# Attention outputs stored as the accumulator leaves them, divided by their sums in the output projection

## The chip, the cores and the metric

The kernel runs on one core of one Trainium2 chip. The metric is the device time of one execution in microseconds. Before the change it is 2662.52 us, the median of 3 runs (2662.07 to 2663.43).

## What is computed

The input x is [4, 2048, 256] in fp32. With xn its layer norm, the result is x + attention(xn) + ffn(xn). The feed-forward part quantises activations and weights to FP4 in blocks of 16 and is not touched. Attention has 16 heads of 16 elements, rotary positions and a causal mask:

```python
q = _rope(q); k = _rope(k)
scores = jnp.einsum('bhqd,bhkd->bhqk', q, k) * scale
scores = jnp.where(causal, scores, jnp.finfo(scores.dtype).min)
attn = jax.nn.softmax(scores, axis=-1)
out = jnp.einsum('bhqk,bhkd->bhqd', attn, v)
return out.transpose(0, 2, 1, 3).reshape(B, S, D) @ Wo.T
```

## The kernel before

Three stages follow each other, each a block of its own in which all engines start together. norm_ffn_qkv leaves x plus the feed-forward result in SBUF (x_all) and q, k, v in DRAM. attention leaves one output per head group in DRAM (oscr). out_projection multiplies by Wo, adds x_all and stores.

Attention has 16 iterations: 4 groups of 4 heads times 4 batches. The queries of an iteration form 4 blocks of 512. For each block of keys at or under the diagonal there is a step. TensorE writes transposed scores (128 keys x 512 queries) for 4 heads into 3 banks (L1013, with a mask matmul at L1018 on the diagonal), ScalarE takes exponentials (L1089), and TensorE weighs v with them into one accumulator bank (L1033). Each head fills 32 rows of it, 16 of values and 16 that hold the sum of the weights, since v is padded with ones.

Softmax needs a row maximum first. TensorE computes the scores a second time, queries as rows, into a ring of 4 banks ("tile", L988), and VectorE reduces them (L1161, with the mask L1166). The maxima are split into three bf16 parts by GpSimd, turned by TensorE (L999), copied by VectorE (L1183), and placed by SyncE as extra rows of q (L929). Part of these tiles belongs to the next iteration.

When a block's accumulator is complete, ScalarE copies it to acc_sb (L1094). TensorE turns it with four transposes into a bank of the same ring (L1043). VectorE takes reciprocals of the sums (L1190) and multiplies (L1193), and SyncE stores 128 x 256 values (L921). This is an "out".

A string of letters, ORDER, sets one order that all engines follow: s is the next score or weighing step, t the next tile of the maxima, r the turn of a row, o an out. Each engine takes from this plan what concerns it. SyncE's queue follows it too, and each DMA waits there in order.

The last stage loads 512 rows of outputs at a time (L1258), turns each 128 x 256 tile with two transposes (L1287), ScalarE copies it (L1313), TensorE projects it with two fp32 matmuls (L1295), VectorE adds x_all (L1329), SyncE stores (L1270). Loads wait until the tile before has been turned.

## Time and profile before

| | |
|---|---|
| profiled execution | 2663.43 us |
| its span | 2661.6 us |
| TensorE matmul busy | 2495.5 us (94%) |
| VectorE busy | 2259.2 us (85%) |
| ScalarE busy | 1629.7 us (61%) |
| GpSimd busy | 73.4 us (3%) |
| mean DMA rate | 59 GB/s |

The span is what the profile covers of the execution; the time is a little longer. In the profile PE is TensorE's matmul, PEld its weight loads, DVE VectorE, ACT ScalarE, POOL GpSimd and SPq SyncE's queue. A busy TensorE is a modelled value, since matmuls are pipelined: one starts before the one ahead has ended. Distances between starts say what it really takes. fp32 matmuls leave two records each, transposes one.

### The profile page before, as it was taken

The numbers are of one execution on the slowest core, as the hardware profiler recorded it, in microseconds if no ns is written. First come the engines' busy times: TensorE is split into PE (matmuls) and PEld (weight loads), VectorE is DVE, ScalarE is ACT, GpSimd is POOL, SyncE is SP. The second block draws the span as 40 slices with busy tenths as digits, with TensorE's granted clock in tenths as the row PEclk, the third lists the DMA queues.
The fourth block names the chain that finished last, engine by engine and source line by source line (L and its number), as shares of the span: only waits on it lengthen the run. The fifth ranks groups of instructions, "written<-read, shape, count | busy, mean of one in ns | idle before, by whom it ended". The sixth has DMA issues, their size and how long they took to land. (4 is left out here: it accounts for less than half of the span.)

```text
span 2661.6 us, 55085 instructions
## 1 busy us (share of the span) xinstructions
PE 2495.5 (94%) x14690; PEld 1210.8 (45%) x14690; DVE 2259.2 (85%) x4939; ACT 1629.7 (61%) x3325; POOL 73.4 (3%) x263
## 2 busy tenths in 40 slices
PE   3699999999998799999999999999999999999979
PEld 1355555655555144344344344444444443433337
DVE  6889889889998798898888889888888988988803
ACT  2355445454553077777777777777777777767752
POOL 0000000000000100000000000000000000000000
PEclk9799999999999599999999999999999999999999
DMA  5021112112211502111112112012011111110017
GB/s 183 32 71 57 65 67 71 58 60 71 71 50 67 140 26 64 28 53 59 36 47 65 30 53 65 23 59 63 26 59 44 44 59 30 51 53 6 7 41 216
DMA packets 168616, 157.81 MB, mean 59 GB/s; under 512 B 47216, under 2 KB 147312, under 8 KB 168432
## 3 DMA queue, kind: packets, MB, share of 16 engines
q1 hardware_dynamic: 168288, 155.10, 19.2%
q8 instruction: 114, 1.87, 0.3%
q14 instruction: 70, 0.57, 0.1%
q10 hardware_dynamic: 144, 0.26, 0.0%
HBM read 95.81 MB, written 58.72 MB: 58 GB/s over the span
## 5 line engine op out<-in xcount | busy, mean ns | idle before, releaser
L1089 ACT ACTIVATE prob<-score 128x512 f32<-128x512 f32 (+3 forms) x2560 | 1158.6, 542 | 472.0 <-PE score L1018 252.1
L1161 DVE TENSOR_REDUCE top<-tile 128x1 f32<-128x512 f32 x1536 | 956.5, 682 | 98.8 <-PE tile L988 92.0
L1013 PE MATMUL score<-qs,ks 99*128 99x512 bf16 (+3 forms) x2560 | 810.9, 351 | 7.1 <-ACT prob L1089 3.1
L988 PE MATMUL tile<-ks,qs 96*128 96x512 bf16 (+3 forms) x2560 | 785.9, 356 | 22.7 <-DMA ks<-qkp 14.8
L1033 PE MATMUL acc<-prob,vs 128*32 128x512 f32 (+3 forms) x5120 | 537.9, 535 | 0.0
L1166 DVE CUSTOM_DVE_ANT_0 tile<-tile,mask 128x128 f32<-128x128 f32 (+3 forms) x1024 | 471.3, 520 | 57.1 <-PE tile L988 41.1
L1013 PEld LDWEIGHTS score<-qs,ks 99*128 99x128 bf16 x2560 | 246.3, 97 | 395.8 <-ACT prob L1089 209.1
L988 PEld LDWEIGHTS tile<-ks,qs 96*128 96x128 bf16 x2560 | 236.3, 98 | 318.4 <-DVE top L1161 101.5
L362 PE MATMUL gu<-wguT,xT 128*128 128x512 f32 (+1 forms) x768 | 315.0, 563 | 20.1 <-DVE hid L670 20.1
L1033 PEld LDWEIGHTS acc<-prob,vs 128*32 128x32 f32 x5120 | 130.3, 109 | 242.9 <-issue 139.3
L362 PEld LDWEIGHTS gu<-wguT,xT 128*128 128x128 f32 x768 | 145.2, 193 | 167.7 <-issue 125.2
L1018 PE MATMUL score<-identb,maskb 128*128 128x128 bf16 x1024 | 214.6, 221 | 3.4 <-issue 3.4
L398 PE MATMUL misc<-wdT,hT 128*128 128x256 f32 x768 | 184.8, 392 | 1.3 <-ACT hT L463 1.3
L398 PEld LDWEIGHTS misc<-wdT,hT 128*128 128x128 f32 x768 | 148.4, 197 | 33.1 <-issue 11.3
L1166 DVE DVE_READ_ACCUMULATOR2_ANT top<- 128x1 f32 x1024 | 143.5, 140 | 1.7 <-issue 1.7
L386 PE MATMUL misc<-xT,wqkvT_sb 128*128 128x512 f32 x256 | 119.3, 610 | 7.6 <-ACT xT L463 7.6
L1018 PEld LDWEIGHTS score<-identb,maskb 128*128 128x128 bf16 x1024 | 101.2, 99 | 48.0 <-issue 2.5
L468 ACT ACTIVATE magic<-scaled 128x704 f32<-128x704 f32 (+1 forms) x96 | 71.1, 741 | 74.4 <-DVE scaled L124 74.4
L483 ACT ACTIVATE silu<-gu 128x704 f32<-128x704 f32 x64 | 48.4, 757 | 102.3 <-PE gu L362 102.3
L133 DVE SCALAR_TENSOR_TENSOR scaled<-magic,scaled 128x704 f32<-128x704 f32 (+1 forms) x96 | 78.7, 820 | 30.4 <-ACT magic L468 29.8
L463 ACT COPY hT<-misc 128x512 f32<-128x512 f32 (+1 forms) x128 | 58.1, 482 | 64.4 <-PE misc L394 63.8
L394 PE MATMUL misc<-identf_sb,hq 128*128 128x128 f32 x384 | 59.5, 278 | 33.3 <-DVE hq L137 28.0
(101 smaller groups left out, 1739.3 us busy)
## 6 DMA issues: line engine op xcount, KB each, us to landing
qkp<-parts SPq DMA_DIRECT2D x192, 128.0 KB
vscr<-vt SPq DMA_DIRECT2D x16, 1024.0 KB, 4.5
vs<-vscr SPq DMA_DIRECT2D x16, 1024.0 KB, 5.7
qs<-qkp SPq DMA_DIRECT2D x64, 192.0 KB, 3.4
ks<-qkp SPq DMA_DIRECT2D x64, 192.0 KB, 3.4
x_all<-in_x SPq DMA_DIRECT2D x16, 512.0 KB, 8.9
qs<-qkp SPq DMA_DIRECT2D x64, 128.0 KB, 3.1
ks<-qkp SPq DMA_DIRECT2D x64, 128.0 KB, 3.1
```

Source lines behind the costliest of these rows:

```text
L133: link(nc.vector.scalar_tensor_tensor(out=scaled, in0=magic, scalar=1.25 * MAGIC, in1=scaled, op0=ALU.max, op1=ALU.add))
L362: mm = nc.tensor.matmul(gu[:, t % 2, c0:c0 + w], xT[:, KT + k, t * P:(t + 1) * P], wguT[:, k, c0:c0 + w], start=(k == 0), stop=(k == KT - 1))
L386: mm = nc.tensor.matmul(bank, wqkvT[:, k, t * P:(t + 1) * P], xT[:, k, :], start=(k == 0), stop=(k == KT - 1))
L398: mm = nc.tensor.matmul(bank[:, 0:DIM], hT[:, t % 2, i, :], wdT[:, i, :], start=(i == 0), stop=(i == IT - 1))
L468: nc.scalar.activation(magic[:, par, 0:w], scaled[:, par, 0:w], ACT.Abs, scale=MAGIC).then_inc(magic_ready, 1)
L988: mm = nc.tensor.matmul(bank[:, h * width:(h + 1) * width], qs[par][0:ROWS, h0 + h, q0:q0 + P], ks[par][0:ROWS, h0 + h, k0:k0 + width], st ...
L1013: mm = nc.tensor.matmul(bank[:, 0:width], ks[par][0:ROWS_M, h, kb * P:(kb + 1) * P], qs[par][0:ROWS_M, h, qb * GROUP + off:(qb + 1) * GROU ...
L1018: mm = nc.tensor.matmul(bank[:, 0:P], maskb[:], identb[:], start=False, stop=True, skip_group_check=True)
L1033: mm = nc.tensor.matmul(acc[h * VW:(h + 1) * VW, off:GROUP], vs[par][:, kb // GT, kb % GT, h, :], prob[:, (HG * n + h) % PROB_SLOTS, 0:GRO ...
L1089: nc.scalar.activation(prob[:, k % PROB_SLOTS, 0:width], score[:, k % SCORE_SLOTS, 0:width], ACT.Exp, scale=HEAD ** -0.5).then_inc(probs_r ...
L1161: nc.vector.tensor_reduce(top[:, j, h0, c:c + 1], bank, AX.X, ALU.max).then_inc(tile_taken, 1)
L1166: last = nc.vector.tensor_tensor_reduce(out=head, in0=head, in1=mask[:, GROUP - width:GROUP], scale=1.0, scalar=MASK, op0=ALU.add, op1=ALU ...
```

## The change

The accumulator goes to DRAM as it is: 128 rows (4 heads x 32) by 512 queries. acc_sb has two halves, and ScalarE's copy waits until the store of two blocks before has landed. Transposes, reciprocal, product and the ring bank of an out are gone. At the letter o only SyncE does something: it stores.

In the last iteration, behind the store of block 1, SyncE loads into the buffers qs0 and ks0, which are free by then, the sums of three batches (12 DMAs) and the turned outputs of 6 of the 16 groups (24 DMAs). When VectorE is through with its iteration it takes the reciprocals of 64 x 1536 sums. GpSimd splits them into three bf16 parts in four passes. After its last store SyncE writes the parts to DRAM and reads those of two batches back as 48 rows, heads times parts.

The last stage starts with the sums of the fourth batch. ScalarE issues the loads of the other 10 groups, 40 DMAs, with no wait. Per group TensorE spreads the reciprocals over 128 rows (two matmuls with a 0/1 matrix of 48 rows), VectorE multiplies the turned outputs by them (2 x 128x512), TensorE projects (8 matmuls), and VectorE adds. There are 4 result buffers in place of 2, and no loop.

```diff
-ORDER = ("stsststtsttssststststsssstststsstssrtsssttstssotststsstsststststtstsststssststststssttsstsssstst"
...
+ORDER = ("stssttsststtssttsstsssstsststsststsssrtststststststostssstststssttststststsststssttsstststssstss"
...
-    uses = [e for e in plan if e[0] in ("tile", "row", "out") and (more or e[0] == "out" or not e[-1])]
+    uses = [e for e in plan if e[0] in ("tile", "row") and (more or not e[-1])]
...
+SUM_ROWS, SPLIT, LAST = QB * HEADS, (BATCH - 2) * QB, (BATCH - 1) * QB
+def load_sums(sp, d, dst, b, loaded):
+    for qb in range(QB):
+        src = d["oscr"][:, b * QB + qb].rearrange("h (k r) c -> h k r c", r=VW)[:, :, HEAD, :]
+        sp.dma_start(dst[qb * HEADS:(qb + 1) * HEADS, :], src).then_inc(loaded, 16)
+def batch_recips(d, p, batches):
+    return d["rscr"][p, batches].rearrange("b g h c -> (g h) b c")
+def turned_groups(flat):
+    return [flat[:, n:n + KT * GROUP].rearrange("p (k c) -> p k c", c=GROUP) for n in range(0, flat.shape[1], KT * GROUP)]
+def load_turned(eng, d, dst, g, k, loaded):
+    for h in range(HGS // KT):
+        src = d["oscr"][k * HGS // KT + h, g].rearrange("(k r) c -> k r c", r=VW)[:, 0:HEAD, :]
+        rows = slice(h * HG * HEAD, (h + 1) * HG * HEAD)
+        eng.dma_start(dst[rows, k, :], src).then_inc(loaded, 16)
+def load_recips(eng, d, recips, b, loaded):
+    for p in range(PARTS):
+        eng.dma_start(recips[p * HEADS:(p + 1) * HEADS], d["rscr"][p, b].rearrange("q h c -> h q c")
+                      ).then_inc(loaded, 16)
+def split_recips(pool, nc, links, base, rest, parts):
+    nc.gpsimd.tensor_copy(parts[0], rest).then_inc(links, 1)
+    pool.wait_ge(links, base + 1)
+    nc.gpsimd.tensor_tensor(rest, rest, parts[0], ALU.subtract).then_inc(links, 1)
+    pool.wait_ge(links, base + 2)
+    nc.gpsimd.tensor_copy(parts[1], rest).then_inc(links, 1)
+    pool.wait_ge(links, base + 3)
+    return nc.gpsimd.tensor_tensor(parts[2], rest, parts[1], ALU.subtract)
...
-        qs = [sb(f"qs{i}", [P, HG, SEQ], BF16) for i in range(2)]
-        ks = [sb(f"ks{i}", [P, HG, SEQ], BF16) for i in range(2)]
+        qs = [qs0, sb("qs1", [P, HG, SEQ], BF16)]
+        ks = [ks0, sb("ks1", [P, HG, SEQ], BF16)]
-        acc_sb = sb("acc_sb", [P, GROUP])
-        recip = sb("recip", [P, GT * HG])
-        ot = sb("ot", [P, 2, GT * HG, HEAD])
+        acc_sb = sb("acc_sb", [P, 2, GROUP])
+        sum_parts = sb("sum_parts", [SUM_ROWS, PARTS, BATCH - 1, GROUP], BF16)
...
-            def store(it, more, e):
-                n, _ = place(it, more, e)
+            def store(it, e):
                 qb = e[1]
-                await_on(sp, sp_passed, tile_taken, n + 1 + TILE_SLOTS)
+                await_on(sp, sp_passed, acc_taken, it * QB + qb + 2)
                 dst = d["oscr"].rearrange("h g p c -> (h g) p c")[ds(it * QB + qb, 1)]
-                sp.dma_start(dst.rearrange("a p c -> (a p) c"),
-                             ot[:, qb % 2].rearrange("p t e -> p (t e)")).then_inc(out_stored[qb % 2], 16)
+                sp.dma_start(dst.rearrange("a p c -> (a p) c"), acc_sb[:, qb % 2, :]).then_inc(out_stored[qb % 2], 16)
                     elif e[0] == "out":
-                        store(it, more, e)
+                        store(it, e)
+                        if more is False and e[1] == 1:
+                            for stored in out_stored:
+                                await_on(sp, sp_passed, stored, it * (QB // 2 * 16) + 1)
+                            await_on(sp, sp_passed, scores_ready, it * HEAD_STEPS)
+                            for b in range(BATCH - 1):
+                                load_sums(sp, d, sums[:, b, :], b, sums_loaded)
+                            for g, dst in enumerate(ahead):
+                                for k in range(KT):
+                                    load_turned(sp, d, dst, g, k, ahead_loaded)
+            await_on(sp, sp_passed, pick_ready, 1)
+            await_on(sp, sp_passed, recips_split, 1)
+            for p in range(PARTS):
+                sp.dma_start(batch_recips(d, p, slice(0, BATCH - 1)), sum_parts[:, p, :, :]).then_inc(recips_stored, 16)
+            await_on(sp, sp_passed, recips_stored, PARTS * 16)
+            for b in range(BATCH - 2):
+                load_recips(sp, d, recips[:, b * QB:(b + 1) * QB, :], b, recips_loaded)
...
-            def out_turn(it, more, e):
-                pe.wait_ge(acc_taken, it * QB + e[1] + 2)
-                bank = tile_slot(it, more, e)
-                for t in range(GT):
-                    mm = nc.tensor.transpose(bank[:, t * P:(t + 1) * P], acc_sb[:, t * P:(t + 1) * P], identf[:])
-                mm.then_inc(tile_full, 1)
...
             def take_acc(it, e):
                 act.wait_ge(pv_done, it * STEPS + e[1] + 1 + PROB_STEPS)
-                nc.scalar.copy(acc_sb[:], acc[:]).then_inc(acc_taken, 1)
+                qb = e[2]
+                act.wait_ge(out_stored[qb % 2], it * (QB // 2 * 16) + qb // 2 * 16 + 1)
+                nc.scalar.copy(acc_sb[:, qb % 2, :], acc[:]).then_inc(acc_taken, 1)
...
+            pool.wait_ge(recips_ready, 1)
+            split_recips(pool, nc, pool_links, ITERS * QB * TOP_LINKS, sums, [sum_parts[:, p] for p in range(PARTS)]
+                         ).then_inc(recips_split, 1)
-            def normalise(it, more, e):
-                qb = e[1]
-                dve.wait_ge(tile_taken, place(it, more, e)[0] + TILE_SLOTS)
-                sums = tile_bank(it, more, e).rearrange("p (t e) -> p t e", e=VW)
-                link(nc.vector.reciprocal(recip[:], sums[:, :, HEAD]))
-                dve.wait_ge(out_stored[qb % 2], it * (QB // 2 * 16) + qb // 2 * 16 + 1)
-                nc.vector.tensor_tensor(ot[:, qb % 2], sums[:, :, 0:HEAD],
-                                        recip[:].unsqueeze(2).broadcast_to([P, GT * HG, HEAD]),
-                                        ALU.mult).then_inc(tile_taken, 1)
...
+            dve.wait_ge(sums_loaded, (BATCH - 1) * QB * 16)
+            nc.vector.reciprocal(sums, sums).then_inc(recips_ready, 1)
+def out_projection(nc, d, x_all, woT, ahead, pickb, recips, out):
+    FIRST = len(ahead)
+    Y_SLOTS = 4
+        spread = ctx.enter_context(nc.psum_tensor("o_spread", [P, 2, KT, GROUP], F32))
+        prod = ctx.enter_context(nc.psum_tensor("o_prod", [P, GT, 512], F32))
+        later = sb("later", [P, (GROUPS - FIRST) * KT * GROUP])
+        attT = ahead + turned_groups(later[:])
+        last_recips = sb("last_recips", [PARTS * HEADS, GROUPS - SPLIT, GROUP], BF16)
+        scaledT = [sb(f"scaledT{i}", [P, KT, GROUP]) for i in range(2)]
+        y = [sb(f"y{i}", [P, GT, DIM]) for i in range(Y_SLOTS)]
...
-            def load(g, par):
-                for h in range(HGS):
-                    src = d["oscr"][h, ds(g, 1)].rearrange("a p (t e) -> p (a t) e", e=OUTW)
-                    sp.dma_start(att[par][:, :, h * OUTW:(h + 1) * OUTW], src).then_inc(att_loaded[par], 16)
...
+            load_sums(sp, d, sums[:], BATCH - 1, sums_loaded)
+            load_recips(sp, d, last_recips[:, 0:QB, :], BATCH - 2, recips_loaded[0])
+            for g in range(GROUPS):
+                if g == 2:
+                    sp.wait_ge(recips_split, 1)
+                    for p in range(PARTS):
+                        sp.dma_start(batch_recips(d, p, slice(BATCH - 1, BATCH)).rearrange("p b c -> p (b c)"),
+                                     sum_parts[:, p, :]).then_inc(recips_stored, 16)
+                if g == 4:
+                    sp.wait_ge(recips_stored, PARTS * 16)
+                    load_recips(sp, d, last_recips[:, QB:2 * QB, :], BATCH - 1, recips_loaded[1])
+                sp.wait_ge(prod_taken, (g + 1) * GT)
+                sp.dma_start(rows[g], y[g % Y_SLOTS][:]).then_inc(y_stored[g % Y_SLOTS], 16)
+            for stored in y_stored:
+                sp.wait_ge(stored, GROUPS // Y_SLOTS * 16)
+        @block.scalar
+        def _(act):
+            for g in range(FIRST, GROUPS):
+                for k in range(KT):
+                    load_turned(act, d, attT[g], g, k, att_loaded[g - FIRST])
+            def spread_recips(g):
+                if g >= SPLIT:
+                    pe.wait_ge(recips_loaded[(g - SPLIT) // QB], PARTS * 16)
+                if g >= 2:
+                    pe.wait_ge(scaled_ready, (g - 1) * KT)
+                recip = recips[:, g, :] if g < SPLIT else last_recips[:, g - SPLIT, :]
                 for k in range(KT):
-                    mm = nc.tensor.transpose(turned[:, t % 2, k * P:(k + 1) * P],
-                                             att[par][:, t % GT, k * P:(k + 1) * P], identf[:])
-                mm.then_inc(turn_full, 1)
-            def project(i, t):
-                pe.wait_ge(turn_taken, i * PAIR + t + 1 + 2)
-                pe.wait_ge(prod_taken, i * PAIR + t + 1)
+                    nc.tensor.matmul(spread[:, g % 2, k, :], pickb[:, k * P:(k + 1) * P], recip,
+                                     start=True, stop=True).then_inc(spread_full, 1)
+            def project(g, t):
+                pe.wait_ge(scaled_ready, (g + 1) * KT)
+                if g:
+                    pe.wait_ge(prod_taken, (g - 1) * GT + t + 1)
                 for k in range(KT):
-                    mm = nc.tensor.matmul(prod[:, t % 2, 0:DIM], attT[:, t % 2, k * P:(k + 1) * P], woT[:, k, :],
+                    mm = nc.tensor.matmul(prod[:, t, 0:DIM], scaledT[g % 2][:, k, t * P:(t + 1) * P], woT[:, k, :],
                                           start=(k == 0), stop=(k == KT - 1))
                 mm.then_inc(prod_full, 1)
+            spread_recips(0)
+            for g in range(GROUPS):
+                if g + 1 < GROUPS:
+                    spread_recips(g + 1)
+                for t in range(GT):
+                    project(g, t)
...
+            def scale(g):
+                if g >= FIRST:
+                    dve.wait_ge(att_loaded[g - FIRST], HGS * 16)
+                if g >= 2:
+                    dve.wait_ge(prod_full, (g - 1) * GT)
+                for k in range(KT):
+                    dve.wait_ge(spread_full, g * KT + k + 1)
+                    nc.vector.tensor_tensor(scaledT[g % 2][:, k, :], attT[g][:, k, :], spread[:, g % 2, k, :],
+                                            ALU.mult).then_inc(scaled_ready, 1)
+            scale(0)
+            scale(1)
+            dve.wait_ge(sums_loaded, QB * 16)
+            nc.vector.reciprocal(sums[:], sums[:]).then_inc(recips_ready, 1)
+            for g in range(GROUPS):
+                if g >= Y_SLOTS:
+                    dve.wait_ge(y_stored[g % Y_SLOTS], g // Y_SLOTS * 16)
+                for t in range(GT):
+                    dve.wait_ge(prod_full, g * GT + t + 1)
+                    nc.vector.tensor_tensor(y[g % Y_SLOTS][:, t, :], prod[:, t, 0:DIM], x_all[:, g * GT + t, :],
                                             ALU.add).then_inc(prod_taken, 1)
+                if g + 2 < GROUPS:
+                    scale(g + 2)
...
+            q_flat, k_flat = (buf[:].rearrange("p h c -> p (h c)").bitcast(F32) for buf in (qs0, ks0))
+            half = k_flat.shape[1] // 2
+            ahead = turned_groups(q_flat) + turned_groups(k_flat[:, 0:half])
+            sums = k_flat[0:SUM_ROWS, half:half + (BATCH - 1) * GROUP].rearrange("p (b c) -> p b c", c=GROUP)
```

The places that the prediction speaks of follow as rows of each engine's program. TensorE in attention, before and after, from the tiles between the accumulators of blocks 1 and 2 on:

```order
L988 MATMUL tile<-ks,qs 128x512
L1011 REGISTER_ALU
L1013 MATMUL score<-qs,ks 128x512
L974 REGISTER_ALU
L1043 MATMUL tile<-identf_sb,acc_sb 128x128 x4
L974 REGISTER_ALU
L988 MATMUL tile<-ks,qs 128x384
```

```order
L1061 MATMUL tile<-ks,qs 128x512
L1084 REGISTER_ALU
L1086 MATMUL score<-qs,ks 128x512
L1084 REGISTER_ALU
L1086 MATMUL score<-qs,ks 128x512
L1047 REGISTER_ALU
L1061 MATMUL tile<-ks,qs 128x384
```

The four transposes of the out are gone, and nothing waits there for the copy. VectorE at the same place, before and after:

```order
L1161 TENSOR_REDUCE top<-tile 128x1
L1188 REGISTER_ALU
L1154 REGISTER_ALU
L1190 RECIPROCAL recip<-tile 128x16
L1193 TENSOR_TENSOR ot<-tile,recip 128x256
L1154 REGISTER_ALU
L1166 ISA tile,top<-tile,mask 128x384
```

```order
L1230 TENSOR_REDUCE top<-tile 128x1
L1223 REGISTER_ALU
L1230 TENSOR_REDUCE top<-tile 128x1
L1223 REGISTER_ALU
L1235 ISA tile,top<-tile,mask 128x384
```

Reductions and masked reductions follow each other directly. SyncE's queue from the last iteration's outs to the first loads of the last stage, before and after:

```order
L921 DMA oscr<-ot 128x256 x2
L929 DMA qs<-row 3x4x128 x4
L921 DMA oscr<-ot 128x256 x2
L839 UNCONDITIONAL_BRANCH
L1251 UNCONDITIONAL_BRANCH
L1258 DMA att<-oscr 128x4x64 x8
```

```order
L975 DMA oscr<-acc_sb 128x512 x2
L823 DMA ks<-oscr 16x1x512 x12
L843 DMA qs<-oscr 64x1x512 x16
L843 DMA ks<-oscr 64x1x512 x8
L982 DMA qs<-row 3x4x128 x4
L975 DMA oscr<-acc_sb 128x512 x2
L1034 DMA rscr<-sum_parts 64x3x512 x3
L849 DMA recips<-rscr 16x4x512 x6
L887 UNCONDITIONAL_BRANCH
L1315 UNCONDITIONAL_BRANCH
L823 DMA last_sums<-oscr 16x1x512 x4
```

36 loads now stand ahead of the row of block 3, and nine DMAs and two waits for landings stand behind the last store.

## Rows read from the trace of the kernel before

**Rows 1.** Table of stretches, busy us (instructions) of PE, PEld, DVE, ACT, POOL; clock, DMA, GB/s:

```profile
1143.00:1245.70 102.70, 102.08 (x726) 42.48 (x726) 92.22 (x242) 75.73 (x166) 4.02 (x16) 1.00 0.17 48
...
2581.30:2586.40 5.10, 4.96 (x14) 3.80 (x15) 0.42 (x1) 1.12 (x3) 0.00 (x0) 0.50 0.34 76
2586.40:2661.60 75.20, 69.09 (x371) 57.99 (x369) 26.76 (x63) 22.04 (x61) 0.00 (x0) 1.00 0.75 209
```

**Rows 2.** Timeline of ScalarE, two accumulator copies (start us, us, instruction):

```profile
1143.04 0.59 ACT L1094 COPY acc_sb<-acc 128x512 f32<-128x512 f32 x1 [0.19 <-PE acc L1033]
...
1348.39 0.59 ACT L1094 COPY acc_sb<-acc 128x512 f32<-128x512 f32 x1 [0.19 <-PE acc L1033]
```

**Rows 3.** Timeline of TensorE around an out in attention:

```profile
1504.10 0.60 PE L1043 MATMUL tile<-identf_sb,acc_sb 128*128 128x128 f32 x4
1504.53 0.38 PE L1013 MATMUL score<-qs,ks 99*128 99x512 bf16 x1
1504.75 0.38 PE L988 MATMUL tile<-ks,qs 96*128 96x512 bf16 x1
...
1505.50 1.92 PE L1033 MATMUL acc<-prob,vs 128*32 128x512 f32 x16
1507.36 0.34 PE L988 MATMUL tile<-ks,qs 96*128 96x384 bf16 x1
```

**Rows 4.** Timeline of VectorE around the same out:

```profile
1504.38 1.27 DVE L1161 TENSOR_REDUCE top<-tile 128x1 f32<-128x512 f32 x2
...
1506.50 0.68 DVE L1161 TENSOR_REDUCE top<-tile 128x1 f32<-128x512 f32 x1
```

**Rows 5.** Waits between 1100 and 2300 us (total us, times, longest):

```profile
PE tile L1043 <- ACT acc_sb L1094: 5.5, 12, 0.5
```

**Rows 6.** Timelines of the last iteration, SyncE's queue and TensorE:

```profile
2507.80 0.33 SPq L921 DMA_DIRECT2D oscr<-ot  x1
2526.96 2.98 SPq L929 DMA_DIRECT2D qs<-row  x4
...
2532.13 0.84 PE L1013 MATMUL score<-qs,ks 99*128 99x512 bf16 x3
```

**Rows 7.** SyncE's issues by line: ns min/median/max, first and last start:

```profile
L929 SPq DMA_DIRECT2D qs<-row x256: 697/699/841, 892.3 to 2529.2; - x128
L899 SPq DMA_DIRECT2D ks<-qkp x192: 563/583/1545, 874.2 to 2366.2; - x192
L921 SPq DMA_DIRECT2D oscr<-ot x64: 332/361/374, 941.6 to 2574.3; - x64
```

**Rows 8.** From attention to the last stage: timeline rows and one of the chain:

```profile
2572.13 0.59 ACT L1094 COPY acc_sb<-acc 128x512 f32<-128x512 f32 x1 [0.55 <-PE acc L1033]
...
2578.36 2.84 DMA att<-oscr
...
2582.55 2.08 PE L1295 MATMUL o_prod<-woT_sb,attT 128*128 128x256 f32 x4
```

**Rows 9.** A projection on the chain that ended last, and the last addition:

```profile
2604.30 0.87 PE o_prod L1295 x4
...
2657.86 0.42 DVE L1329 TENSOR_TENSOR y<-o_prod,x_all 128x256 f32<-128x256 f32 x1 [0.44 <-PE o_prod L1295]
```

**Rows 10.** Groups by line and shape: busy us, mean ns, idle time before:

```profile
L124 DVE SCALAR_TENSOR_TENSOR scaled<-xn,inv 128x512 f32<-128x512 f32 x32 | 22.1, 692 | 1.1
L1190 DVE RECIPROCAL recip<-tile 128x16 f32<-128x16 f32 x64 | 16.5, 257 | 57.6 <-PE tile L1043 52.3
L104 DVE RECIPROCAL inv<-inv 128x96 f32<-128x96 f32 x1 | 0.8, 753 | 0.0
L1329 DVE TENSOR_TENSOR y<-o_prod,x_all 128x256 f32<-128x256 f32 x64 | 27.2, 425 | 56.9 <-PE o_prod L1295 55.3 <-DMA out<-y 1.6
L1131 POOL TENSOR_TENSOR top_parts<-rest,top_parts 128x16 bf16<-128x16 f32 x64 | 17.1, 267 | 11.5 <-POOL top_parts L1129 11.5
L544 POOL MEMSET vt<- 128x2048 f32 x1 | 1.8, 1805 | 0.3 <-POOLq L1378 0.3
```

**Rows 11.** DMA issues by line: KB each, median us to landing:

```profile
vs<-vscr SPq DMA_DIRECT2D x16, 1024.0 KB, 5.7
```

More of the change, by code:

```diff
@@ L50 @@
 ITERS = HGS * BATCH
-OUTW = HG * HEAD
-OT = GT * OUTW
 LEAD = 0.52
@@ L814, in slot_free, with attention @@
     return it * per_iteration + last - per_iteration + 1 + slots
-def attention(nc, d, identf):
+SUM_ROWS, SPLIT, LAST = QB * HEADS, (BATCH - 2) * QB, (BATCH - 1) * QB
[24 more added lines that the diff above has]
+    return nc.gpsimd.tensor_tensor(parts[2], rest, parts[1], ALU.subtract)
+def attention(nc, d, identf, qs0, ks0, ahead, sums, pickb, recips):
     plan, STEPS = attention_plan()
@@ L1059, in iteration @@
                         weigh(it, i, par, e)
-                    elif e[0] == "out":
-                        out_turn(it, more, e)
                     elif e[0] == "tile" and (more or not e[-1]):
@@ L1203, in _ @@
                     take_row(None, None, e)
-            assert not link.n
             def iteration(it, more):
-                link.enter(it * OUT_LINKS)
                 for e in plan:
-                    if e[0] == "out":
-                        normalise(it, more, e)
-                    elif e[0] == "tile" and (more or not e[-1]):
+                    if e[0] == "tile" and (more or not e[-1]):
                         reduce_tile(it, more, e)
@@ L1253, in _ @@
             rows = out.rearrange("(g t p) k -> g p t k", t=GT, p=P)
-            def load(g, par):
-                for h in range(HGS):
-                    src = d["oscr"][h, ds(g, 1)].rearrange("a p (t e) -> p (a t) e", e=OUTW)
-                    sp.dma_start(att[par][:, :, h * OUTW:(h + 1) * OUTW], src).then_inc(att_loaded[par], 16)
-            load(0, 0)
-            load(1, 1)
-            def pair(i, more):
-                for par in range(2):
-                    if more:
-                        await_on(sp, sp_passed, turn_full, i * PAIR + GT * (par + 1) + 2)
-                        load(i * 2 + 2 + par, par)
-                    await_on(sp, sp_passed, prod_taken, i * PAIR + GT * (par + 1) + 2)
-                    sp.dma_start(rows[ds(i * 2 + par, 1)].rearrange("a p t k -> p (a t) k"), y[par][:]
-                                 ).then_inc(y_stored[par], 16)
@@ L1297, in project @@
                 mm.then_inc(prod_full, 1)
-            with pe.Fori(0, GROUPS // 2) as i:
-                for t in range(PAIR):
-                    turn(i, t)
-                    if t:
-                        project(i, t - 1)
-                project(i, PAIR - 1)
-        @block.scalar
-        def _(act):
-            with act.Fori(0, GROUPS // 2) as i:
-                for t in range(PAIR):
-                    act.wait_ge(turn_full, i * PAIR + t + 1 + 2)
-                    act.wait_ge(prod_full, i * PAIR + t + 1)
-                    nc.scalar.copy(attT[:, t % 2, :], turned[:, t % 2, 0:DIM]).then_inc(turn_taken, 1)
+            spread_recips(0)
@@ L1315, in _ @@
+            for g in range(GROUPS):
[3 more added lines that the diff above has]
+                    project(g, t)
         @block.gpsimd
         def _(pool):
-            for s, n in ((turn_full, 2), (turn_taken, 2), (prod_full, 2), (prod_taken, 2), (y_stored[0], 1),
-                         (y_stored[1], 1)):
-                pool.sem_inc(s, n)
+            pool.wait_ge(recips_ready, 1)
+            split_recips(pool, nc, split_links, 0, sums[:], [sum_parts[:, p, :] for p in range(PARTS)]
+                         ).then_inc(recips_split, 1)
@@ L1340, in program @@
         norm_ffn_qkv(nc, d, x_all, woT, identf)
-        attention(nc, d, identf)
-        out_projection(nc, d, x_all, woT, identf, out)
+        with nc.sbuf_tensor("qs0", [P, HG, SEQ], BF16) as qs0, nc.sbuf_tensor("ks0", [P, HG, SEQ], BF16) as ks0, \
+                nc.sbuf_tensor("pickb", [PARTS * HEADS, DIM], BF16) as pickb, \
+                nc.sbuf_tensor("recips", [PARTS * HEADS, SPLIT, GROUP], BF16) as recips:
+            q_flat, k_flat = (buf[:].rearrange("p h c -> p (h c)").bitcast(F32) for buf in (qs0, ks0))
+            half = k_flat.shape[1] // 2
+            ahead = turned_groups(q_flat) + turned_groups(k_flat[:, 0:half])
+            sums = k_flat[0:SUM_ROWS, half:half + (BATCH - 1) * GROUP].rearrange("p (b c) -> p b c", c=GROUP)
+            attention(nc, d, identf, qs0, ks0, ahead, sums, pickb, recips)
+            out_projection(nc, d, x_all, woT, ahead, pickb, recips, out)
 def constants():
```

74 lines of the change are left out of this document (35 added, 39 removed).

## The prediction

> **What bounds the kernel now.** The order of reading was: the table of stretches, the timelines of TensorE and VectorE inside attention, the waits, then the end. The table gives one steady iteration of attention: 102.70 us with TensorE busy 102.08, VectorE 92.22, ScalarE 75.73 [rows 1]. The copy of the last block's accumulator stands at 1143.04 and two iterations later at 1348.39 [rows 2], so one takes 205.35 / 2 = 102.7 us. There are 16, some 1640 of the 2661.6 us; from the last accumulator copy [rows 8] to the span's end are 89.5.
>
> TensorE's busy time is modelled, so its load is counted from distances between starts. A 512-column bf16 matmul follows the next after 0.22 us (1504.53 to 1504.75), the sixteen records of two weighing steps take 1.86 (1505.50 to 1507.36), the four transposes 0.43 (1504.10 to 1504.53) [rows 3]. Per iteration scores and maxima have 69,632 columns each, 272 x 0.22 = 59.8 us; 64 mask matmuls at a quarter of that, 3.5; 24 full weighing steps x 0.93 = 22.3; 16 diagonal ones at 5/8 of the columns, 9.3; four out-turns, 1.7. That is 96.6 of 102.7: TensorE truly idles 6 us, VectorE 10.5. Neither is the bound alone; they meet in a ring of four banks, and VectorE runs dry while TensorE weighs. The two floors are close, so removed work counts only in part.
>
> After attention, the last accumulator copy starts at 2572.13 and the first projection at 2582.55 [rows 8]; then 64 tiles follow until the last addition at 2657.86 [rows 9], 75.3 us, TensorE bound: four projection records take 0.87 [rows 9] and two transposes 0.22, 1.09 a tile against 75.3 / 64 = 1.18 measured.
>
> **Part 1: attention loses the out-turn.** Each of 64 blocks loses four transposes on TensorE (0.43 us) and a reciprocal and a product on VectorE. On VectorE two reductions run from 1504.38 for 1.27 and the next starts only at 1506.50 [rows 4]: the pair occupies 2.12 - 1.27 = 0.85 us. If TensorE alone bounds, the gain is 63 x 0.43 = 27 us, plus its waits for the copy before a transpose, 5.5 us in 1200 [rows 5], 7 us in all: 27 to 34. If VectorE alone bounds, 60 x 0.85 = 51 us and, with the slot hand-overs around it, at most 55. TensorE is the nearer to full, so I start from its 34 and add 6: VectorE's relief is 3.4 us an iteration, which is twice TensorE's own 1.7, so some of TensorE's 6 us of waiting for a bank or a probability goes too. I take 40 us, 2.5 an iteration, ends 27 and 55. The new order of letters keeps 200 steps of scores and weighing and 140 tile letters; runs of three tiles fall from 6 to 5 and runs of two rise from 17 to 22. I price it at nothing, with ends inside those of this part and one rival. The last two outs lie in the last iteration, where VectorE is free.
>
> ScalarE's copy now waits for the store of two blocks before. Behind it on ScalarE stand all exponentials. The store is issued as soon as the copy is done, its issue costs 0.36 us [rows 7], and two blocks later is 31 us or more on, apart from the short block 0; I cost it at nothing. SyncE's store waits for the copy instead of VectorE, so it is earlier.
>
> **Part 2: SyncE's queue in the last iteration.** After the store of block 1, 12 small loads and 24 of 128 KB are issued ahead of the row of block 3. Before, this gap went from 2507.80 to 2526.96, 19.2 us, the scores that need the row start at 2532.13, and the row's own four issues take 2.98 [rows 6]. The trace has no such issue; its neighbours are 0.36, 0.58 and 0.70 us [rows 7], so 36 take 13, 21 or 25 us. The store itself now comes some 3 us earlier. At 0.58 the row is placed in time; at 0.70 it is 3 us late and eats the slack. Taken 0, ends 0 and 5 us.
>
> **Part 3: the reciprocals of three batches.** SyncE places the last row at 2526.96 [rows 6], right behind VectorE's last copy of the iteration, so VectorE is free from 2527. A reciprocal costs 257 ns for 16 elements and 753 for 96 [rows 10], 6.2 ns each; 1536 elements take 9.7 us, done by 2537. Then four GpSimd passes over 64 x 1536. GpSimd shows 267 ns for 16 elements and 1805 for a fill of 2048 [rows 10]. Scaled by length, that is 1.4 us or 25.6 us a pass, 5 to 102 in all. I take the row of near length, doubled for the second operand, some 11 us. SyncE asks for the result near 2573, so 36 us are free and anything up to 9 us a pass costs nothing. The Trainium skill, "GPSIMD Engine Reference", section 3.1, gives 4497 ns for a two-input fp32 pass over 2048; as an estimate from that page a pass here takes 3.4 us and four 13.5, also hidden. No row here shows it.
>
> **Part 4: the hand-over.** From the start of the copy: copy 0.6, store issue 0.4, three reciprocal stores at 0.58 (1.7), landing 2.8 as the load at 2578.36 [rows 8], six loads at 0.58 (3.5), less one overlap, landing 2.8, block change 0.3: about 11 us, so TensorE starts near 2583. It spreads two halves at half speed (0.44 each; the granted clock was 0.50 between 2581.3 and 2586.4, the 1.2 GHz level, after 8 us without work [rows 1]) and VectorE scales them, 0.69 us each, the price of a 512-column fp32 pass [rows 10]. First projection at 2585.2, 2.7 us later than before; ends 1 and 5.
>
> **Part 5: the last stage.** Per group TensorE has 2 x 0.22 for spreading and 4 x 0.87, 3.92 us against 4.71 measured now (75.3 / 16). VectorE has 2 x 0.69 + 4 x 0.43 = 3.1, beside it. ScalarE leaves the path. But VectorE does a reciprocal of 64 x 512 between its second scaling and the first addition: 257 ns + 496 x 6.2 = 3.3 us, after sums that land near 2587.3, so until 2590.7. Group 0 has four product banks, so TensorE stands until 2591.2. Then 15 groups x 3.92 less a spreading already done = 58.4 us, so the last addition starts near 2649.5 against 2657.86. Gain of parts 4 and 5 together, rounded for the waits between: 8.5 us, ends 4 and 12.
>
> **Sum.** 40 + 8.5 = 48.5 us off the profiled execution's 2663.43, 2614.9; that execution is 0.9 above the median of 2662.52, so about 2614 as a median. What a measurement here can tell from no change is about 0.2%, 5 us.
>
> **Rivals.**
> TensorE alone is the bound in attention, VectorE's relief only lengthens its idle time: 27 + 8.5, so 2627. For it: 96.6 of 102.7 filled. Against: the waits for banks.
> VectorE's slot counts whole: 55 + 8.5, so 2599. For it: each weighing step leaves TensorE ahead by its ring only. Against: VectorE idles 10.5 us already.
> The last stage becomes bound by transfers: it now asks for 40 loads x 128 KB = 5.2 MB from ScalarE's queue at once, beside 8.4 MB of results. At the 209 GB/s of the present stage [rows 1] that is 65 us, just what TensorE needs. At 1024 KB in 5.7 us, 184 GB/s [rows 11], it is 74, and the stage gains nothing: 2623. Against: DMA was busy 0.75 with rows of 256 bytes, now they are 2 KB. The Trainium skill, "DMA: Bandwidth & Descriptors", section "Issuing engines are not separate DMA queues", says that DMAs issued from several engines share the same 16 engines and save only issue time. By that rule the loads from ScalarE slow the stores of SyncE, and this rival is more likely than two queues suggest.
> The new order loses what the lighter engines win (2.5 us an iteration more waiting at the ring): 8.5 only, 2654.
> On the other side: the GpSimd split is slow. At 25.6 us a pass it ends near 2639, 66 us after SyncE asks, and the second split (64 x 512, a third of it, 34 us) then holds SyncE at group 2 with the results of that group, some 20 us more with four result buffers. 2662.5 - 48.5 + 66 + 20 = 2700. It decides from 9 us a pass on, and makes the kernel slower from some 20. For it: GpSimd's only arithmetic rows are short. Against: its fill of 2048 elements ran at 0.9 ns each.
>
> **How the numbers follow.** Forecast 0.56, TensorE alone 0.16, VectorE whole 0.11, transfers 0.07, order 0.04, GpSimd 0.06. The predicted time is 2614. The likeliest case has 2603 to 2624; the range reaches to 2597 for the VectorE case and to 2636 for TensorE alone with a late row and a late hand-over, leaving out the order and GpSimd cases. Faster by over 0.2%: all but the last and part of the order case, 0.91; within: 0.03; slower: 0.06.
>
> **What would show it.** The distance of the accumulator copies over two iterations should fall from 205.35 to about 200.4. VectorE busy per iteration should be near 89.5 and TensorE's idle time between 5 and 6. The GpSimd passes over 1536 elements should take 1.4 to 5 us and end before the last copy. First projection 13 us after the start of the last copy. Groups in the last stage 3.9 us apart, with one gap of 1 to 3 us before group 1. Wrong would be: groups over 4.3 apart with VectorE waiting for loads or stores, a TensorE wait for the row of block 3 in the last iteration, or an iteration above 101.5.

## The result and the profile after

The changed kernel takes 2654.45 us, the median of 10 runs (2652.05 to 2657.97); the kernel before took 2662.29 beside it. The ratio is 0.9971, 95% interval 0.9961 to 0.9981. It is faster by about 8 us, where 48.5 were forecast and 2597 was the range's lower end, 2636 its upper.

The account needs three marks: the copy of block 3's accumulator in the last iteration but one, the last copy, the span's end.

| | before | after | gained |
|---|---|---|---|
| copy of block 3, iteration 14 (from 0) | 2473.27 | 2441.44 | 31.8 |
| from there to the last copy | 98.9 | 115.6 | -16.7 |
| last copy to the span's end | 89.5 | 96.8 | -7.3 |
| span | 2661.6 | 2653.8 | 7.8 |

The first mark before, in ScalarE's timeline:

```profile
2473.27 0.59 ACT L1094 COPY acc_sb<-acc 128x512 f32<-128x512 f32 x1 [0.55 <-PE acc L1033]
```

Timeline of ScalarE after, the two copies that answer to [rows 2], and those of the account:

```profile
1138.18 0.58 ACT L1162 COPY acc_sb<-acc 128x512 f32<-128x512 f32 x1 [0.19 <-PE acc L1106]
1339.62 0.58 ACT L1162 COPY acc_sb<-acc 128x512 f32<-128x512 f32 x1 [0.19 <-PE acc L1106]
2441.44 0.58 ACT L1162 COPY acc_sb<-acc 128x512 f32<-128x512 f32 x1 [0.71 <-PE acc L1106]
2557.05 0.58 ACT L1162 COPY acc_sb<-acc 128x512 f32<-128x512 f32 x1 [0.55 <-PE acc L1106]
```

An iteration of attention takes 201.44 / 2 = 100.7 us against 102.7: 2 us gained of the 2.5 forecast. Of the 40.7 us that are missing from the forecast gain of 48.5, 8.2 are missing in the first line of the table (31.8 instead of 40), 16.7 in the second, and 15.8 in the third (a loss of 7.3 instead of a gain of 8.5). SyncE's queue after, in the last iteration, which answers to [rows 6] (start us, us from the first issue's start to the last one's end, count):

```profile
2472.85 0.33 SPq L975 DMA_DIRECT2D oscr<-acc_sb  x1
2473.43 8.18 SPq L823 DMA_DIRECT2D ks<-oscr  x12
2481.66 13.61 SPq L843 DMA_DIRECT2D qs<-oscr  x16
2495.31 10.24 SPq L843 DMA_DIRECT2D ks<-oscr  x8
2505.67 3.46 SPq L982 DMA_DIRECT2D qs<-row  x4
```

The 36 loads hold the queue for 32 us. VectorE had the row of block 3 ready at 2494.33, but SyncE placed it from 2505.67 on. Its last issue ends at 2509.13, and TensorE goes on only at 2515.90. VectorE's and TensorE's timelines, and the wait between 2441 and 2557 us:

```profile
2494.05 0.28 DVE L1252 CAST row<-tile 48x128 bf16<-48x128 f32 x1 [5.91 <-PE tile L1072]
2515.90 1.46 PE L1086 MATMUL score<-qs,ks 99*128 99x512 bf16 x3 [16.83 <-DMA qs<-row]
```

```profile
PE score L1086 <- DMA qs<-row: 16.8, 1, 16.8
```

So the row is late twice: 11.3 us in being issued, and then, between the last issue's end and the scores, 6.8 us, where r_major (below) needs 1.1 (2501.36 to 2502.45). What moves in most of that time is the loads. DMA traffic after between 2509.13 and 2514.5 us (packets, MB, share of 16 engines):

```profile
q1 hardware_dynamic: 283, 0.55, 26.3%
```

In the trace's packets the last 2 KB of the loads end at 2514.83, and the row's own packets, of 256 bytes, run from 2514.56 to 2514.96. The 16.8 us are nearly all of the second line of the table: in loads_behind (below), which has no such wait, the last iteration takes 97.6 us. Another 1 us or so goes behind the wait, where the granted clock is 0.50, the 1.2 GHz level, until 2519.4.

In the last stage the issues of the same load by line (ns min/median/max, first and last start), then DMA issues of that stage (KB each, median us to landing) and a wait:

```profile
L843 ACTq DMA_DIRECT2D later<-oscr x40: 537/1799/4024, 2567.9 to 2630.8; - x40
L843 SPq DMA_DIRECT2D qs<-oscr x16: 528/548/1384, 2481.7 to 2494.1; - x16
L843 SPq DMA_DIRECT2D ks<-oscr x8: 1164/1208/1452, 2495.3 to 2504.4; - x8
```

```profile
out<-y SPq DMA_DIRECT2D x16, 512.0 KB, 8.5
```

```profile
DVE scaledT L1385 <- DMA later<-oscr: 11.9, 3, 4.7
```

ScalarE needs 62.9 us from the first to the last start of 40 issues, so the last loads come late. On the chain that ended last stands one of these loads, `later<-oscr`, with 13.65 us to landing.

### The profile page after: what moved, and what is told of

Its sections match the earlier page's. It is cut to its first block and busy times, and to the rows that moved or that the text cites. A ratio compares the mean times of both kernels' runs of the same rounds, so it can differ in the third digit from the quotient of the medians.

```text
span 2653.8 us, 53527 instructions
## 1 busy us (share of the span) xinstructions
PE 2456.0 (93%) x14338; PEld 1176.3 (44%) x14338; DVE 2250.4 (85%) x4845; ACT 1603.0 (60%) x3262; POOL 85.9 (3%) x271
## 5 line engine op out<-in xcount | busy, mean ns | idle before, releaser
L1086 PE MATMUL score<-qs,ks 99*128 99x512 bf16 (+3 forms) x2560 | 815.0, 351 | 39.3 <-DMA qs<-row 16.8
L1061 PE MATMUL tile<-ks,qs 96*128 96x512 bf16 (+3 forms) x2560 | 776.8, 355 | 23.0 <-DMA ks<-qkp 14.2
L396 PEld LDWEIGHTS misc<-wdT,hT 128*128 128x128 f32 x768 | 149.4, 198 | 33.1 <-issue 11.3
```

The lines of the kernel that those rows point to most:

```text
L396: mm = nc.tensor.matmul(bank[:, 0:DIM], hT[:, t % 2, i, :], wdT[:, i, :], start=(i == 0), stop=(i == IT - 1))
L1061: mm = nc.tensor.matmul(bank[:, h * width:(h + 1) * width], qs[par][0:ROWS, h0 + h, q0:q0 + P], ks[par][0:ROWS, h0 + h, k0:k0 + width], st ...
L1086: mm = nc.tensor.matmul(bank[:, 0:width], ks[par][0:ROWS_M, h, kb * P:(kb + 1) * P], qs[par][0:ROWS_M, h, qb * GROUP + off:(qb + 1) * GROU ...
```

## The experiments

All kernels start from the changed one, except where said. "Iteration" is the distance of two block-3 copies two iterations apart, halved. The kernel before took 2661.11 us beside them (2662.29 beside the changed kernel). Iterations and the last column are read from the profiled execution of each run.

| run | us | ratio to before, 95% | iteration | last copy to end of span |
|---|---|---|---|---|
| changed kernel | 2654.45 | 0.9971 [0.9961, 0.9981] | 100.7 | 96.8 |
| r_major | 2630.75 | 0.9887 [0.9870, 0.9903] | 100.7 | 86.1 |
| loads_behind | 2638.90 | 0.9916 [0.9900, 0.9933] | 100.7 | 96.2 |
| two_heads_load, one run | 2710.39 | | 100.7 | 152.7 |
| old_order | 2678.68 | 1.0064 [1.0047, 1.0081] | 102.2 | 97.1 |
| new_order_before | 2666.84 | 1.0017 [1.0007, 1.0026] | 103.1 | 89.2 |
| dve_back, one run | 2664.96 | | 101.6 | 96.9 |
| pe_back, one run | 2706.81 | | 102.7 | 115.8 |
| repaired | 2620.39 | 0.9846 [0.9833, 0.9859] | 100.7 | 80.6 |

**r_major: the axis order of one load.** The 128 KB load walks its source as 4 heads x 16 rows x 512. Here the rows come first, with the rows of Wo and the 0/1 matrix reordered to match. Bytes, DMAs and their places stay.

```diff
-        src = d["oscr"][k * HGS // KT + h, g].rearrange("(k r) c -> k r c", r=VW)[:, 0:HEAD, :]
+        src = d["oscr"][k * HGS // KT + h, g].rearrange("(k r) c -> r k c", r=VW)[0:HEAD, :, :]
...
-    head_of = np.arange(DIM) // HEAD
+    head_of = np.arange(DIM) // (HG * HEAD) * HG + np.arange(DIM) % HG
...
-        "woT": np.asarray(L0_attn_Wo).T,
+        "woT": np.asarray(L0_attn_Wo).T.reshape(HGS, HG, HEAD, DIM).transpose(0, 2, 1, 3).reshape(DIM, DIM),
```

> One edit to the changed kernel: the turned outputs are loaded with the row within a head as the slowest dimension (16 x 4 rows) in place of the head (4 x 16 rows), with the rows of Wo and of the 0/1 matrix in the same order. Bytes, number of DMAs and row length stay. Theory A, few engines: a load whose slowest dimension is 4 runs on 4 DMA engines, so its queue fills and each issue waits. Then with 16 the issues on SyncE fall from 0.85 and 1.27 us apart to about 0.6, the 36 loads take some 22 us in place of 32, the wait for the row of block 3 falls from 16.8 to 6 to 8 us, the 40 issues of ScalarE take 22 to 28 us in place of 64.6, the stores of results land in 3 to 4 us in place of 8.5, and the waits for loads in the last stage (11.9 us) are gone: 2654.5 - 9 - 12 = about 2633. Theory B, shared traffic: loads and stores slow each other by their bytes alone. Then the issue distances stay near 1.8 us and the time within 3 us of 2654.

It is 23.7 us faster than the changed kernel (22 by the ratios to the kernel before). Issues by line of r_major, DMA issues of its last stage, and its wait for the row:

```profile
L843 ACTq DMA_DIRECT2D later<-oscr x40: 603/616/1404, 2553.9 to 2582.2; - x40
L843 SPq DMA_DIRECT2D qs<-oscr x16: 588/594/600, 2482.1 to 2491.6; - x16
```

```profile
out<-y SPq DMA_DIRECT2D x16, 512.0 KB, 3.1
later<-oscr ACTq DMA_DIRECT2D x40, 128.0 KB, 3.9
```

```profile
PE score L1086 <- DMA qs<-row: 3.0, 1, 3.0
```

ScalarE's median goes from 1799 to 616 ns, no addition or scaling waits for a load, and the wait for the row falls from 16.8 to 3.0. The bytes are the same, so theory B, shared traffic by bytes alone, is out: the axis order is the cause. A fixed price of 1.8 us for each DMA on ScalarE's queue (theory C of two_heads_load) is out as well, since the same 40 DMAs are now issued in 28.3 us.

The medians of the stores, 8.5 and 3.1 us, can't be compared as they stand, since in r_major the loads are soon done and most stores run alone. Stores issued while loads were under way, in r_major (2564 to 2586 us) and in the changed kernel (2580 to 2628), then those behind the loads in both (2586 to 2630, 2642 to 2654):

```profile
out<-y SPq DMA_DIRECT2D x6, 512.0 KB, 4.6
out<-y SPq DMA_DIRECT2D x12, 512.0 KB, 9.1
out<-y SPq DMA_DIRECT2D x10, 512.0 KB, 2.9
out<-y SPq DMA_DIRECT2D x2, 512.0 KB, 2.9
```

Sharing does slow a store, with either order, and more beside the slow loads. In neither kernel does an addition wait for a store.

**loads_behind: the queue alone.** The 36 loads are issued behind the row of block 3.

```diff
-                    elif e[0] == "out":
-                        store(it, e)
-                        if more is False and e[1] == 1:
+                        if more is False and e[1] == QB - 1:
...
+                    elif e[0] == "out":
+                        store(it, e)
```

> One edit to the changed kernel: the 36 loads of the last iteration are issued behind the row of block 3 and not ahead of it. The loads themselves stay. Theory A, order in SyncE's queue: the wait of TensorE for the row (16.8 us) goes and nothing takes its place, since the loads end long before attention does; 2654.5 - 16 to 17 = 2638. Rival: the row's own DMAs are slow because the loads still hold the same DMA engines, or another wait for something SyncE does (the store of block 2) appears; then less than 8 us come back, 2647 or more.

SyncE's queue of loads_behind:

```profile
2490.30 2.98 SPq L982 DMA_DIRECT2D qs<-row  x4
2493.55 8.16 SPq L823 DMA_DIRECT2D ks<-oscr  x12
2501.75 13.58 SPq L843 DMA_DIRECT2D qs<-oscr  x16
2515.37 10.24 SPq L843 DMA_DIRECT2D ks<-oscr  x8
```

The row is placed 15.4 us sooner, its wait is gone, and the last iteration takes 97.6 us (2437.31 to 2534.91) instead of 115.6. The loads still issue at the same slow pace, so this gives back the second line of the table and leaves the third. By the medians it is 15.6 us. The profiled execution, 2632.97, is 6 us below the other three (2638.68 to 2639.14), so its parts do not add up to the median.

**two_heads_load: smaller in the same way.** ScalarE's loads are cut into two of two heads, 64 KB each. If the first axis sets the pace, halving it must hurt though the bytes stay.

```diff
-        eng.dma_start(dst[rows, k, :], src).then_inc(loaded, 16)
...
+            for j in range(2):
+                eng.dma_start(dst[h * 64 + j * 32:h * 64 + j * 32 + 32, k, :], src[2 * j:2 * j + 2]).then_inc(loaded, 16)
```

> The changed kernel with each load of the last stage's 10 groups cut into two of 64 KB with two heads each, so the slowest dimension is 2. Same bytes, 80 DMAs in place of 40. Theory A, engines by the slowest dimension: half as many engines carry the same bytes, so the rate of the loads halves, from 5.2 MB in 76 us to about 5.2 MB in 130 to 150, and the stage gets 50 to 75 us longer: 2705 to 2730. Theory B, shared traffic by bytes: no change, 2654. Theory C, a fixed price of each DMA on ScalarE's queue (1.8 us each): 80 x 1.8 = 144 us, also some 2730; it is told apart by the run with the row slowest, where C keeps 1.8 us a load.

Issues by line and a wait of two_heads_load:

```profile
L847 ACTq DMA_DIRECT2D later<-oscr x80: 620/1200/3949, 2566.6 to 2684.6; - x80
```

```profile
DVE scaledT L1389 <- DMA later<-oscr: 36.9, 4, 9.8
```

The same 5.2 MB take 118 us to issue: 62.9 with a first axis of 4, 118 with 2, 28.3 with 16. The traffic of ScalarE's queue in the last stage shows why: packets, MB and the packets' own time as a share of 16 engines' time, in the changed kernel (2557 to 2654 us), two_heads_load (2556 to 2709) and r_major (2543 to 2630):

```profile
q10 hardware_dynamic: 2720, 5.24, 14.1%
q10 hardware_dynamic: 2720, 5.24, 8.9%
q10 hardware_dynamic: 3200, 5.25, 21.5%
```

2560 of these packets are the rows of 2 KB. The others have 4 bytes each: 160 for 40 DMAs, 160 for 80, 640 for 40, which is 4, 2 and 16 a DMA, the first axis each time. A packet is not slower with the heads first: the packets' own time sums to 14.1% of 16 x 97 = 219 us, to 218 in two_heads_load, and to more, 299, in r_major. So a slower walk through memory is not the reason either. What differs is how many run at once. From the starts and durations of the 2 KB packets it is 2.9 on the mean in the changed kernel, 1.7 in two_heads_load and 9.1 in r_major, and it is at most 4 in 97%, at most 2 in 95% and at most 16 in 96% of the time.

**old_order and new_order_before: the letters.** The first is the changed kernel with ORDER of before; the second the kernel before with the new ORDER.

> The changed kernel with the order of letters of the kernel before. Theory A, the new order is worth something in attention: an iteration is longer than 100.72 us, by 0.3 to 1.0, some 5 to 15 us in all. Rival, the order is worth nothing here: iterations within 0.2 us of 100.72. The last iteration moves too: the store of block 1 comes 4 score steps earlier and the row of block 3 two letters earlier, so the wait for the row may change by 1 to 3 us.

> The kernel before, with its out-turn, and the new order of letters as the only edit. In the changed kernel the new order is worth 1.50 us an iteration (102.20 to 100.70), the missing out-turn under the old order 0.46 (102.66 to 102.20). Theory A, the order is worth its 1.5 by itself: iterations near 101.2, 2662 - 22 = 2640. Theory B, the order only pays together with the lighter engines, since it was made for them: iterations at 102.2 to 103.5, 2655 to 2675.

With the old letters, taking the out-turn away gains only 0.5 us an iteration (102.7 to 102.2) and the whole kernel is slower than before. With the new letters it gains 2.4 (103.1 to 100.7). The new letters by themselves cost the kernel before 0.4. "Priced at nothing" was off by 1.5 us an iteration in the changed kernel, and the two edits cannot be priced apart.

**dve_back and pe_back: which engine's relief.** VectorE's share of an out and TensorE's are put back singly. In pe_back VectorE also copies one column, to give the bank of the ring back.

```diff
...
+                    if e[0] == "out":
+                        link(nc.vector.reciprocal(spare_recip[:], spare[:, :, 0]))
+                        link(nc.vector.tensor_tensor(spare[:], spare[:],
+                             spare_recip[:].unsqueeze(2).broadcast_to([P, GT * HG, HEAD]), ALU.mult))
```

```diff
...
+            def out_turn(it, more, e):
+                pe.wait_ge(acc_taken, it * QB + e[1] + 2)
+                bank = tile_slot(it, more, e)
+                for t in range(GT):
+                    mm = nc.tensor.transpose(bank[:, t * P:(t + 1) * P], acc_sb[:, e[1] % 2, t * P:(t + 1) * P], identf[:])
+                mm.then_inc(tile_full, 1)
...
+                    if e[0] == "out":
+                        dve.wait_ge(tile_taken, place(it, more, e)[0] + TILE_SLOTS)
+                        nc.vector.tensor_copy(spare[:], tile_bank(it, more, e)[:, 0:1]).then_inc(tile_taken, 1)
```

> The changed kernel, in which VectorE again does a reciprocal of 128 x 16 and a product of 128 x 256 at each out, on a scratch tile in SBUF that nobody waits for; no transposes, no ring bank. Theory A, both engines count: 0.9 us each time, iterations at 101.5 to 103. Theory B, TensorE alone bounds an iteration: within 0.3 us of 100.70. Theory C, VectorE alone: 100.70 + 3.4 = 104.1.

> The changed kernel, in which TensorE again turns the stored accumulator with four transposes into a bank of the ring at each out, and VectorE only copies one column of it to give the bank back (0.1 to 0.2 us); the result isn't used. Theory B, TensorE alone bounds: 100.70 + 1.7 to 2.2 = 102.4 to 102.9 an iteration. Theory A, both count: 101.5 to 103. Theory C, VectorE alone: within 0.7 of 100.70.

VectorE's work costs 0.9 us an iteration, transposes with their ring bank 2.0. Both are more than nothing and their sum, 2.9, exceeds the 2.4 that the pair costs. So neither engine alone is the bound. pe_back is no clean share of TensorE: its four copies of 0.16 us put 0.6 us an iteration on VectorE. pe_back's long last stage is its own: at block 3 VectorE waits for the turned bank before it starts the three batches' reciprocals. VectorE's timeline of pe_back, behind ScalarE's last accumulator copy at 2589.11:

```profile
2590.52 0.16 DVE L1276 COPY spare<-tile 128x1 f32<-128x1 f32 x1 [37.17 <-PE tile L1117]
2590.59 9.73 DVE L1290 RECIPROCAL ks<-ks 64x1536 f32<-64x1536 f32 x1
```

That is a side effect of the experiment; only its iteration is used.

**repaired: both mends, and the reciprocals' trip earlier.** r_major and loads_behind together, and SyncE stores and reads back the reciprocals of three batches behind the store of block 2 instead of behind the last one.

```diff
...
+                        if more is False and e[1] == QB - 2:
+                            await_on(sp, sp_passed, pick_ready, 1)
+                            await_on(sp, sp_passed, recips_split, 1)
+                            for p in range(PARTS):
+                                sp.dma_start(batch_recips(d, p, slice(0, BATCH - 1)), sum_parts[:, p, :, :]).then_inc(recips_stored, 16)
+                            await_on(sp, sp_passed, recips_stored, PARTS * 16)
+                            for b in range(BATCH - 2):
+                                load_recips(sp, d, recips[:, b * QB:(b + 1) * QB, :], b, recips_loaded)
```

> The changed kernel with three edits: loads with the row slowest (16 x 4), the 36 loads behind the row of block 3, and the reciprocals of the first three batches stored and read back behind the store of block 2, where SyncE waits anyway, not behind the last one. Theory: the remaining 3.0 us of waiting for the row go, the hand-over from the last accumulator copy to the first projection falls from 12.9 us to 6 to 8, and the last stage keeps the pace of 4.2 us a group: 2630.8 - 3 - 5 to 6 = 2622. Rival: the last stage then waits for the sums of the fourth batch as long as the hand-over gets shorter, 2626.

It is 34 us faster than the changed kernel and 41 faster than before. Timelines of repaired at the hand-over:

```profile
2537.93 0.59 ACT L1163 COPY acc_sb<-acc 128x512 f32<-128x512 f32 x1 [0.55 <-PE acc L1107]
...
2542.72 5.25 PE L1359 MATMUL o_prod<-woT_sb,scaledT 128*128 128x256 f32 x16 [0.73 <-DVE scaledT L1386]
...
2551.38 5.38 PE L1359 MATMUL o_prod<-woT_sb,scaledT 128*128 128x256 f32 x16 [2.87 <-DVE y L1398]
```

The first projection comes 4.8 us after the last copy instead of 12.9, which is 8.1 sooner. The stage gets only 5.5 us shorter than in r_major. The wait for the last batch's reciprocal before the second group stays, 2.9 us against 1.1 in r_major, and the second group takes 5.38 us instead of 3.69, since the granted clock is 0.50 again from 2552.7 to 2556.1, behind that wait.

## Why the prediction was wrong

Two of the three signs of being wrong that the prediction names came: a TensorE wait for the row of block 3, and groups over 4.3 us apart with VectorE waiting for loads. The third, an iteration above 101.5, did not.

**Part 1, attention.** 31.8 us of the forecast 40, inside its ends of 27 and 55. Of these, 25.3 are 13 steady iterations, 2.3 lie ahead of them, and 4.2 in the step from iteration 13 to 14, 2 more than an even step gives (see what stays open). The mechanism held: two engines near full, relief of one counting in part. The price of the order did not: the text put the new letters at nothing, so that the removal alone would bring 2.5 us. The runs show 0.5 under the old order and 2.4 under the new.

**Part 2, SyncE's queue: the step that failed.** It took 0, with ends 0 and 5 us, from issues at 0.36, 0.58 or 0.70 us and nothing for the transfers of the loads. The queue then was held for 32.2 us, not 13 to 25, the row's data moved only when the loads' had, and 16.8 us of TensorE waiting followed. The 12 loads of sums cost 0.68 us each. The first nine turned ones cost 0.53 to 0.56, below the neighbour of 0.58, the tenth 0.86, and from the eleventh on each takes 1.17 to 1.45. So the price of an issue was right as long as the queue took them, and the step left out that a queue can be held by what its loads still have to move. The neighbours in the table were loads of another pattern and could not show it. With rows first the turned ones stand 0.64 apart but for one, 36 loads hold the queue for 24.4 us, and TensorE waits 3.0 us for the row, the lateness that the text worked out for 0.70.

The Trainium skill, "DMA: Bandwidth & Descriptors", section "Why a DMA increments its semaphore by 16 and not by 1", says that a DMA runs on the largest number of engines up to 16 that divides the slowest axis, leaving out axes of size 1, of both sides. By that rule the load of 4 x 16 x 512 has 4 engines, the cut one 2, and rows first 16. The trace names no engine for a packet, but the 4, 2 and 16 small packets a DMA and the packets under way at once agree with it. That the issues slow down because few engines drain the queue is argued from this, since no count of what waits in the queue is in the trace.

**Part 3, reciprocals on VectorE and GpSimd.** Right, and hidden. Timelines after of VectorE and GpSimd:

```profile
2494.26 9.73 DVE L1277 RECIPROCAL ks<-ks 64x1536 f32<-64x1536 f32 x1
```

```profile
2504.06 1.46 POOL L856 CAST sum_parts<-ks 64x1536 bf16<-64x1536 f32 x1 [14.22 <-DVE ks L1277]
2505.59 3.08 POOL L858 TENSOR_TENSOR ks<-ks,sum_parts 64x1536 f32<-64x1536 f32 x1
```

9.73 us against 9.7 forecast; four passes of 9.1 us together against 11, done at 2513.35. The rival of a slow GpSimd is out by a factor of 8.

**Part 4, the hand-over.** Right: the first projection starts 12.9 us after the last copy, forecast 13.

**Part 5, the last stage.** Timeline of TensorE and VectorE after:

```profile
2569.93 5.73 PE L1358 MATMUL o_prod<-woT_sb,scaledT 128*128 128x256 f32 x16
2575.91 3.35 DVE L1391 RECIPROCAL last_sums<-last_sums 64x512 f32<-64x512 f32 x1 [4.84 <-DMA last_sums<-oscr]
2579.68 5.38 PE L1358 MATMUL o_prod<-woT_sb,scaledT 128*128 128x256 f32 x16 [3.48 <-DVE y L1397]
2585.52 3.72 PE L1358 MATMUL o_prod<-woT_sb,scaledT 128*128 128x256 f32 x16
2589.17 0.60 PE L1350 MATMUL o_spread<-recips,pickb 48*128 48x512 bf16 x2
2589.70 3.72 PE L1358 MATMUL o_prod<-woT_sb,scaledT 128*128 128x256 f32 x16
```

The reciprocal takes 3.35 us (forecast 3.3) and TensorE stands 3.5 before the second group (forecast 1 to 3). A group takes 4.18 us where nothing is late, not 3.92: 3.65 for the projections against 4 x 0.87, and 0.53 for spreading against 0.44. Over 15 groups that is 3.9 of the missing gain. r_major, free of late loads, ends 86.1 us after its last copy, 3.4 less than before where 8.5 were forecast: below the lower end of 4. The other 10.7 us up to 96.8 are mostly the late loads. The last two groups start 7.3 us each behind the one before, against 4.2 and 3.6 in r_major: 6.8 us. The sums of the fourth batch land later beside the slow loads (VectorE waits 4.8 us for them, 2.9 in r_major), which makes the wait before the second group 2 us longer. Behind that wait the granted clock is 0.50 from 2580.9 to 2584.3, and the second group takes 5.38 us instead of 3.69.

**The rivals.** The transfer rival (2623) named the right place and the wrong mechanism: it saw bytes and a shared rate, and the shared traffic theory fell in r_major. Stores did land later beside the loads, as it said, but nothing waited for one. The rival of the order (2654) has the measured number and not the cause, since attention did gain its 31.8 us and the new letters gain 1.5 us an iteration where they were to lose 2.5. Agreement of a total says nothing about its terms.

**What stays open.** The step from iteration 13 to 14 is longer than an even one, and how much varies between kernels (110.1 us before, 105.9 after, 102.9 in loads_behind). Some 3 us of it go with the clock. The changed kernel, r_major and repaired have 6.8 us at a granted clock of 0.50 in it and take 105.7 to 105.9; loads_behind and two_heads_load have 1.00 throughout and take 102.9 and 103.0. In the changed kernel the stretch begins in a gap of 2.4 us in TensorE's work. As in [rows 1]:

```profile
2386.30:2393.10 6.80, 5.92 (x25) 1.55 (x26) 3.13 (x14) 1.22 (x3) 0.00 (x0) 0.50 0.00 1
```

loads_behind has nearly the same gap, 2.3 us, and no such stretch, and no run tells why. The kernel before has a gap of 3.4 us and 6.8 us at 0.50 behind it, and why its step takes 4.2 us more than the changed kernel's was not tested. Why the pairs of dve_back and pe_back add up to more than both together was not tested either.

## What to carry to other kernels

Before a DMA gets a price, look at the first axis of its access pattern (here the 4 heads of the source), and take its duration only from a DMA of the same pattern; if there is none, the bound is open on the far side. Price what the queue has to move as well as what it has to issue. Name what stands behind it in its queue: here a row of four DMAs with 3 KB each paid 16.8 us for 128 KB loads. Where two engines meet in a small ring, price the removed work together with the instruction order that goes with it, by one run of each order if that can be had.

## What the runs showed of the hardware that was not expected

- The issue time of a DMA depends on its pattern once some are under way. With 4 heads x 16 rows the first nine take 0.53 to 0.56 us on SyncE's queue and the later ones 1.17 to 1.45, the median on ScalarE's queue is 1.80. With 16 rows x 4 heads nearly all take 0.6 on both queues, with the same bytes and the same 2 KB rows.
- A load leaves 4, 2 or 16 packets of 4 bytes beside its data, as its first axis has 4, 2 or 16 entries, and mostly no more than that many of its queue's packets run at once.
- The row's data stood 5.4 us behind its last issue (2509.13 to 2514.56) until the loads ahead in the same queue had moved.
- Such loads also slow the stores of another queue: 9.1 us for 512 KB beside them, 4.6 beside loads with rows first, 2.9 alone.
